# A graph network on one core: the one-hot of the edge sort, its engines, and the order of the index preparation

## The reference

```python
# block 0: two graph attention layers on layer_norm(x), then a linear map of [x, out2]
h = (x_norm @ W1).reshape(n, 4, 192)
s_src, s_dst = (h * a_src1).sum(-1), (h * a_dst1).sum(-1)
e = leaky_relu(s_src[src] + s_dst[dst]);  alpha = softmax of e over the edges of one dst
out1 = segment_sum(alpha * h[src], dst) + b1          # the same again with W2, 2 heads of 96
x = layernorm(x + concat(x, out2) @ Wu + bu)
# block 1: relational convolution (34 relations), then a graph convolution
mean = segment_sum(x[src], type * n + dst) / count    # one mean per relation and node
h1 = einsum(mean, W_rel) + x @ W_root + b
x = layernorm(x + normalised_adjacency(src, dst) @ (h1 @ W_gcn) + b)
```

## Time and profile before

| | |
|---|---|
| three runs | median 3916.02 us (3913.81 to 3950.95) |
| the profiled execution | 3912.97 us |
| its span | 3911.2 us, 67870 instructions |
| mean granted TensorE clock | 0.94 |
| busy | PE 90%, DVE 51%, ACT 37%, POOL 36% of the span |
| first VectorE instruction of the sort | at 96.27 us |
| first VectorE instruction behind the sort (L971) | at 277.02 us |
| chain that ended last, by engine | PE 70%, DVE 14%, issue 6% |

### The profile page before, as it was taken

The page is one execution under the profiler, slowest core; times in us unless marked ns, Lnnn a source line. Parts: engine busy times, 40 slices in busy tenths (PEclk is TensorE's granted clock), DMA queues, the critical chain, the costliest instruction groups (busy, mean ns, idle before and its releaser), DMA issues.

```text
span 3911.2 us, 67870 instructions
## 1 busy us (share of the span) xinstructions
PE 3508.4 (90%) x19011; PEld 2237.3 (57%) x19011; DVE 2004.9 (51%) x4523; ACT 1449.5 (37%) x2473; POOL 1417.5 (36%) x1878
## 2 busy tenths in 40 slices
PE   6889977958999999999999999999999987667778
PEld 4334457857566666666666666666666654444445
DVE  7999997856522122122123454454454326666564
ACT  2765534625122222222223444444443323333330
POOL 0760000000055544444303444444443206677661
PEclk9999977979999999999999999999999997778889
DMA  2000000011143333333334555555544434444441
GB/s 81 1 1 0 0 10 1 1 36 56 58 145 102 103 113 103 102 113 103 101 115 138 157 163 166 167 164 166 162 159 143 141 120 140 123 127 125 127 105 55
DMA packets 224476, 390.32 MB, mean 100 GB/s; under 512 B 38885, under 2 KB 179172, under 8 KB 224398
## 3 DMA queue, kind: packets, MB, share of 16 engines
q1 hardware_dynamic: 164942, 246.72, 18.6%
q0 software_dynamic: 57600, 141.81, 13.4%
q10 hardware_dynamic: 1856, 0.79, 0.1%
HBM read 250.79 MB, written 138.41 MB: 100 GB/s over the span
## 4 chain that ended last, share of the span: by engine, by line
PE 70%; DVE 14%; issue 6%; DVEq 2%; ACT 2%; DMA 2%; another core or an unknown queue 2%; POOL 1%; SPq 0%; ACTq 0%; POOLq 0%
PE bank L1554 17%; PE bank L1556 17%; PE bank L1555 17%; PE bank L1438 3%; PE bank L1545 3%; PE bank L1546 3%; PE bank L1611 3%; DVE arena L1001 3%; PE bank L1529 2%; DVE arena L1037 2%; PE bank L1332 1%; DVE arena L1000 1%; PE bank L1621 1%; DVE agg_lo L1207 1%
## 5 line engine op out<-in xcount | busy, mean ns | idle before, releaser
L1554 PE MATMUL bank<-arena 128*128 128x384 f16 (+1 forms) x4200 | 1384.5, 330 | 3.1 <-issue 2.2
L1555 PE MATMUL bank<-arena 128*128 128x384 f16 (+1 forms) x4200 | 1382.2, 329 | 4.1 <-issue 4.1
L1556 PE MATMUL bank<-arena 128*128 128x384 f16 (+1 forms) x4200 | 1381.2, 329 | 3.4 <-issue 3.4
L811 ACT ACTIVATE arena<-bank,winv 128x384 f32<-128x384 f32 (+1 forms) x680 | 391.0, 579 | 1327.1 <-PE bank L1556 967.8
L573 POOL DMA_INDIRECT arena<-y_half,idx_now x720 | 764.7, 1062 | 284.5 <-issue 174.4
L1554 PEld LDWEIGHTS bank<-arena 128*128 128x128 f16 (+2 forms) x4200 | 425.9, 101 | 285.6 <-issue 34.5
L1556 PEld LDWEIGHTS bank<-arena 128*128 128x128 f16 (+2 forms) x4200 | 425.5, 101 | 272.1 <-issue 16.1
L1555 PEld LDWEIGHTS bank<-arena 128*128 128x128 f16 (+2 forms) x4200 | 426.2, 101 | 265.0 <-issue 15.3
L801 ACT ACTIVATE agg_hi<-arena,typ_s 128x384 fp32r<-128x384 f32 x720 | 406.8, 608 | 446.4 <-remote 138.2
L1207 DVE SCALAR_TENSOR_TENSOR agg_lo<-arena,typ_s,agg_hi 128x384 fp32r<-128x384 f32 x720 | 442.3, 614 | 159.4 <-ACT agg_hi L801 80.1
L1545 PE MATMUL bank<-agg_hi,agg_oh 128*128 128x384 f32 x720 | 307.7, 427 | 179.0 <-DVE agg_lo L1207 137.5
(11 more groups left out here) (213 smaller groups left out, 3646.4 us busy)
## 6 DMA issues: line engine op xcount, KB each, us to landing
y_half<-arena SPq DMA_DIRECT2D x612, 192.0 KB
arena<-in_L_gnn_W_rel_dram SPq DMA_DIRECT2D x68, 1152.0 KB
arena<-y_half,idx_now POOLq DMA_INDIRECT x720
y_half<-arena SPq DMA_DIRECT2D x68, 147.0 KB
w_now<-rel_inv_dram,idx_now POOLq DMA_INDIRECT x360, 2.7
arena<-in_x_dram SPq DMA_DIRECT2D x10, 384.0 KB, 3.5
arena<-in_L_gnn_b_rgcn_dram SPq DMA_DIRECT2D x10, 384.0 KB
x_dram<-arena SPq DMA_DIRECT2D x9, 384.0 KB, 2.6
```

The lines of the kernel that those rows point to most:

```text
L811: nc.scalar.activation(to, bank[n % RB][0:r, 0:CH], ACT.Copy, scale=winv[0:r, c:c + 1]).then_inc(r_copied, 1)
L1554: nc.tensor.matmul(acc, xh, w_hi[c][:, k, :], start=(k == 0), stop=False)
L1555: nc.tensor.matmul(acc, xh, w_lo[c][:, k, :], start=False, stop=False)
L1556: ins = nc.tensor.matmul(acc, xl, w_hi[c][:, k, :], start=False, stop=(k == KT - 1))
```

## The change

- The lane one-hot takes the payload `one_f` in the same instruction: `(iota == lane) * one_f`. Slot 0 of the ring holds this product, and a slot has two planes instead of three.
- ScalarE makes the second plane from the first, multiplying by `two_f / one_f`; VectorE computes that ratio in the index preparation with two more instructions (`reciprocal`, `tensor_tensor`).
- GpSimd has no part in the sort any more; the semaphore `oh_lane` is gone, and TensorE waits for two semaphores a column instead of three.
- The W1 attention columns are built behind the index preparation, directly in front of VectorE's sort loop, by another form: one fused multiply and sum of 192 elements for each head (`tensor_tensor_reduce`), 48 in all, with two buffers `prod`, each waiting for the group but one before it.
- TensorE's order: the two matmuls that clear the sort's banks stand in front of all products; 2 products (H_EARLY) stand in front of the partition sums, 8 behind them, all of the first half of the columns; the ten of the second half stand behind parts 1 to 10 of the sort, and `w1a_ready` is waited for behind part 0.
- The three index arrays are loaded by ScalarE's queue, ahead of its four vectors, and no longer by SP behind `x`.

```diff
-        oh_l = view(V0, [NL, 3, P], F16)
+        oh_l = view(V0, [NL, 2, P], F16)
...
-        prod = view(V0 + 18432, [D])
+        prod = [view(V0 + 12288 + i * D * 4, [D]) for i in range(2)]
...
-        H_EARLY = 6
-        H_FIRST = 12
-        H_ORDER = ([(n, 0) for n in range(H_EARLY)] + [(n, 1) for n in range(H_EARLY)]
-                   + [(n, q) for n in range(H_EARLY, NT) for q in range(HALVES)])
+        H_EARLY = 2
+        H_FIRST = NT
+        H_ORDER = [(n, q) for q in range(HALVES) for n in range(NT)]
...
         @block.sync
-            for t, v in ((dst, dst_i), (src, src_i), (etype, typ_i)):
-                sp.dma_start(v, t.rearrange("(p c) -> p c", p=EP)).then_inc(idx_loaded, 16)
...
         @block.gpsimd
-            with pool.Fori(0, EC // NL) as i:
-                for k in range(NL):
-                    c = i * NL + k
-                    pool.wait_ge(oh_lane, c + 1)
-                    nc.gpsimd.tensor_tensor(oh_l[0:EP, k, 2, :], oh_l[0:EP, k, 0, :],
-                                            two_f[:, bass.ds(c, 1)].broadcast_to([EP, P]), ALU.mult).then_inc(oh_two, 1)
...
         @block.scalar
+            for t, v in ((dst, dst_i), (etype, typ_i), (src, src_i)):
+                act.dma_start(v, t.rearrange("(p c) -> p c", p=EP)).then_inc(idx_loaded, 16)
...
-                        act.wait_ge(oh_lane, c + 1)
+                        act.wait_ge(oh_one, c + 1)
                         nc.scalar.activation(oh_l[0:EP, k, 1, :], oh_l[0:EP, k, 0, :], ACT.Copy,
-                                             scale=one_f[:, at]).then_inc(oh_one, 1)
+                                             scale=two_f[:, at]).then_inc(oh_two, 1)
...
         @block.vector
-            dve.wait_ge(w1_loaded, 16)
-            dve.wait_ge(vec_loaded, 64)
-            for k in range(KT):
-                for j, a in enumerate((a1s, a1d)):
-                    after(nc.vector.tensor_tensor(prod, W1s[:, k, 0:D], a, ALU.mult))
-                    ins = nc.vector.tensor_reduce(W1s[:, k, D + j * H1:D + (j + 1) * H1],
-                                                  prod.rearrange("p (h c) -> p h c", h=H1), AX.X, ALU.add)
-                    after(ins)
-            nc.vector.memset(prod[:, 0:1], 0.0).then_inc(w1a_ready, 1)
...
             after(nc.vector.tensor_scalar(two_f, two_f, float(-HALF), None, ALU.add))
+            after(nc.vector.reciprocal(dloc_f, one_f))
+            after(nc.vector.tensor_tensor(two_f, two_f, dloc_f, ALU.mult))
...
             nc.vector.tensor_copy(unit_bucket[:, :], bu_f).then_inc(units_ready, 1)
 
+            dve.wait_ge(w1_loaded, 16)
+            dve.wait_ge(vec_loaded, 64)
+            w1a_done = []
+            for k in range(KT):
+                for j, a in enumerate((a1s, a1d)):
+                    if len(w1a_done) >= 2:
+                        dve.wait_ge(dve_seq, w1a_done[-2])
+                    for h in range(H1):
+                        o = slice(h * C1, (h + 1) * C1)
+                        ins = nc.vector.tensor_tensor_reduce(prod[j][:, o], W1s[:, k, o], a[:, o], 1.0, 0.0, ALU.mult, ALU.add,
+                                                             W1s[:, k, D + j * H1 + h:D + j * H1 + h + 1])
+                    w1a_done.append(seq.add(ins))
+            dve.wait_ge(dve_seq, w1a_done[-1])
+            nc.vector.memset(prod[0][:, 0:1], 0.0).then_inc(w1a_ready, 1)
...
-                    nc.vector.tensor_scalar(oh_l[0:EP, k, 0, :], iota[0:EP, 0:P], lane_f[:, at], None,
-                                            ALU.is_equal).then_inc(oh_lane, 1)
+                    nc.vector.tensor_scalar(oh_l[0:EP, k, 0, :], iota[0:EP, 0:P], lane_f[:, at], one_f[:, at],
+                                            ALU.is_equal, ALU.mult).then_inc(oh_one, 1)
...
         @block.tensor
+            for f in range(2):
+                ins = nc.tensor.matmul(bank[f][:, 0:ET], zeros[:, :], iota[:, 0:ET], start=True, stop=True)
+            ins.then_inc(oh_free, NL)
             pe.wait_ge(w1_loaded, 16)
             for i in range(H_EARLY):
                 h_product(i)
...
-            pe.wait_ge(w1a_ready, 1)
             for i in range(H_EARLY, H_FIRST):
                 h_product(i)
 
-            for f in range(2):
-                ins = nc.tensor.matmul(bank[f][:, 0:ET], zeros[:, :], iota[:, 0:ET], start=True, stop=True)
-            ins.then_inc(oh_free, NL)
...
-                        pe.wait_ge(oh_one, c + 1)
                         pe.wait_ge(oh_two, c + 1)
                         for f in range(2):
-                            ins = nc.tensor.matmul(bank[f][:, 0:ET], oh_l[0:EP, k, 1 + f, :], oh_t[0:EP, k, :],
+                            ins = nc.tensor.matmul(bank[f][:, 0:ET], oh_l[0:EP, k, f, :], oh_t[0:EP, k, :],
                                                    start=False, stop=False, skip_group_check=True)
                         ins.then_inc(oh_free, 1)
+                if m == 0:
+                    pe.wait_ge(w1a_ready, 1)
                 for i in h_with(m):
                     h_product(i)
```

More of the change, by code:

```diff
@@ L181, in program @@
         NL = 15
-        oh_l = view(V0, [NL, 3, P], F16)
+        oh_l = view(V0, [NL, 2, P], F16)
         oh_t = oh_t[:, 0:NL * ET].rearrange("p (s t) -> p s t", s=NL)
-        assert EC % NL == 0 and NL * 3 * P * 2 <= 18432
+        assert EC % NL == 0 and NL * 2 * P * 2 <= 12288
         CB = 2
@@ L249, in program @@
         part_tot, part_psum = sem("part_tot"), sem("part_psum")
-        oh_lane, oh_ready, oh_one, oh_two, oh_free = (sem(n) for n in (
-            "oh_lane", "oh_ready", "oh_one", "oh_two", "oh_free"))
+        oh_ready, oh_one, oh_two, oh_free = (sem(n) for n in ("oh_ready", "oh_one", "oh_two", "oh_free"))
         sort_psum, sorted_ready = sem("sort_psum"), sem("sorted_ready")
```

## The result

The changed kernel takes 3882.89 us (median of 4 executions, 3878.89 to 3890.48), the one before in the same sessions 3914.91. The medians lie 32 us apart, 0.8%. The ratio estimated from all executions is 0.9879, with a 95% interval of 0.9832 to 0.9926; it is not the quotient of the medians (0.9918), which lies inside the interval. So the kernel is faster, by 0.7% to 1.7%.

A forecast was written before the change was run, and what follows sets the result against it. VectorE was taken to set the pace up to the decoding at 277.02 us. Savings of 16.5 us in the head and 28.5 in the sort, 44.9 in all, brought the span from 3911.2 to 3866.3; forecast 3871, range 3858 to 3892.

The forecast's parts named there:

- column 0.446: Sort: VectorE's two one-hots for one column take 0.446 us in place of 0.53, 147.2 us in all.
- GpSimd as the cause of the slow one-hots: Old sort: GpSimd's work beside VectorE slows a one-hot by about 0.14 us.
- 0.06 us for an operand: Sort: each operand given per partition adds 0.06 us to a VectorE instruction, a column going from 0.385 to 0.446.
- rival A: Sort: the second operand is free, a column is 0.385 and TensorE the bound, 146 us, time 3865; chance 0.17.
- Rivals B and C: Sort: fused form loses the fast mode, 3904 us, chance 0.09; slow one-hots not due to GpSimd, 3919 us, chance 0.05.
- I take 0.8 us: Head: index loads ahead of or beside `x` delay the normalising by 0.8 us, 2.5 at most.
- a delay of up to 7 us there is hidden: Head: ScalarE's vectors land some 17 us into the span and are needed only at about 24 us.
- the wait for the sums: Head: VectorE waits for TensorE's partition sums from 46.7 to 48.6 us, 1.9 us.
- rival D: Head: the fused reductions for the W1 columns take 0.44 us each and not 0.28, 7.7 us later, 3879; chance 0.08.
- behind that, each microsecond won is passed on unchanged: Behind the decoding, at 277.02 us before: the same engines start the same work in the same order, so the whole gain arrives.
- The chance of 0.71: Whole kernel: chance of a time below 3877 us, the line for "faster"; 0.25 for the same, 0.04 for slower.
- The slower rival: Sort: TensorE falls to 1.2 instead of 2.4 GHz, some 4006 us if for the whole sort; chance 0.03.

The follow-up runs named there:

- the two operand kernels: The changed kernel with constant 1.0 for `one_f` in the lane one-hot, or with a column of ones multiplied into the tile one-hot: sort 146.1 and 172.2 us.
- the second pair: The changed kernel profiled once more on the first chip, unaltered, against the same profile of the kernel before: 3878.13 us, ratio 0.9875.
- the third chip: Another chip, where the unaltered changed kernel and the kernel before were run again: 3776.99 us against 3820.93, ratio 0.9865.

## Why the prediction was right, and where it was off

**The bound and the place.** Right: everything is won between 0 and the decoding, 42.4 us of 44.9 forecast. The two halves were 12.7 to 14.0 us in the head (16.5 forecast) and 28.5 in the sort (28.5 forecast).

**The sort, 152.3 us forecast, 152.3 measured.** Each step of it was tested by itself: column 0.446 (measured 0.446), GpSimd as the cause of the slow one-hots (put back, 0.18 us for each product), 0.06 us for an operand (less: 0.39; more: 0.507), TensorE nearly level and the 146 us of rival A once the operand is gone (146.1). Rivals B and C fall with the 0.446. Rival A and the cycle table of the Trainium skill (VectorE: DVE Perf Modes, section on the TRN2 errata), which has no term for such an operand, are refuted by the two operand kernels.

**The head, 79.8 us forecast, 82.3 measured.** The order of the steps was right, three terms of the sum were too small; the start of the sort itself scatters by 0.8 us (82.3 to 83.1). "I take 0.8 us" for the index loads: it was 3.6, beyond even the 2.5 called the most; the bound by bytes left out that `x` begins to arrive later, too (VectorE's first statistics at 7.27 us). Of ScalarE's vectors it says that "a delay of up to 7 us there is hidden": `a_dst` landed 12.8 us later than before (10.83 + 19.0 against 2.54 + 14.5, the issue in the timeline of the kernel before below), as it was issued 8.3 us later and took 4.5 longer, and held the transposes' copy-out from about 28 to 29.87. Both are gone with the loads on SP. And 0.5 us between the last fused reduction (68.4 + 13.4 = 81.8) and the first one-hot had no term. Against them the first two products were quicker than the 10.3 us that I had used (9.01 for 24 records), and the wait for the sums was 1.24 us and not 1.9.

```profile
2.54 0.72 ACTq L625 DMA_DIRECT2D arena<-in_L_gnn_a_dst_dram  x1
```

**The fused reductions, 0.28 us forecast, 0.28 measured.** The row at 1250 elements carried over to 192, and rival D falls. The rule of the Trainium skill, (N + 151) / 0.96 ns in the section on the TRN2 errata of VectorE: DVE Perf Modes, gives an estimated 0.36 and matches the record's own length (0.36), not the distance of starts, which is what a chain of them costs.

**The sum, 3871 forecast, 3883 measured.** The step that failed is "behind that, each microsecond won is passed on unchanged". It holds to about 2300 us in this pair of profiles and not for the rest: 10 of 42 us were missing at the end, 4 of 40 in the second pair. At least 6 us of this is scatter; the rest of it is open. On the third chip 4.4 were lost in front of x1, at the lower clock level, and next to nothing behind it. Two sets of four executions of the changed kernel have medians 4.8 us apart, so one such set can't settle the last 5 us. The range, 3858 to 3892, had been drawn for costs in the sort and in the head, and held the time for another reason. That is luck: no term of it stood for a loss behind the sort. The chance of 0.71 for "faster" rested on that number too, 6 us below its own line, and was too high.

**The slower rival** (TensorE at its lower level in the sort) did not come: 0.99 granted in 81.8 to 236 us.

## What to carry to other kernels

Price a VectorE instruction in a chain by the distance of starts and not by its record, and for f16 one-hots like these add 0.06 us for each operand given per partition; and look for VectorE one-hots of two durations beside a GpSimd that is busy, since GpSimd's work here cost VectorE 0.14 to 0.18 us for each product. Once two engines are nearly level (here 147 and 141 us by the prediction's sum), look next at what stands between the last unit of work and the one that waits for it: moving the last product one part forward gave 4 us, and nothing in its profile shows a cost. A gain in the first tenth of a span arrives at its end only as well as what lies behind repeats, so compare the profiles at the point where the change ends before the times.

## What the runs showed of the hardware that I had not expected

- Three loads of 161 KB issued beside `x` on another queue delayed the first use of `x` by 1.8 us (5.49 to 7.27) and its last by 3.6.
- The same program takes 3915 us on one chip and 3820 on two others; up to about 2050 us the profiles of one kernel agree within 5 us (1.1 for the kernel before), and the granted clock over the whole span is 0.941 on the first and 0.951 on the third. Chip and hour changed together, so that it is the chip is likely and not shown.
- The stretch to x1 takes 783.9 to 791.8 us with identical instructions. In the one pair that was followed (786.7 and 791.1), TensorE's lower level falls on other instructions at the two places where time is lost: 8.21 us for 5.70 in one, 5.61 for 4.04 in the other.
